# Turning and splitting the first batch's keys and values while the sorted projection still runs

## The reference, cut to what matters

```python
x = x + 0.5 * _L0_ffn_ref(_layernorm(x), ...)      # stage 1
x = x + _L0_attn_ref(_layernorm(x), ...)
x = x + 0.5 * _L0_ffn_ref(_layernorm(x), ...)      # stage 3

def _L0_ffn_ref(x, ...):
    q = _fff(x, q_...); k = _fff(x, k_...); v = _fff(x, v_...)
    attn = jax.nn.softmax(jnp.einsum('bqd,bkd->bqk', q, k) * scale, axis=-1)
    return jnp.einsum('bqk,bkd->bqd', attn, v)
```

## Time and profile before

| | |
|---|---|
| device time, median of 3 runs | 3100.54 us (3093.82 to 3103.66) |
| the profiled execution: time / span | 3108.3 us / 3106.5 us |
| mean granted clock of PE | 0.952 |
| PE busy over the span | 2852.1 us (92%) |
| DVE / ACT busy | 2122.3 us (68%) / 1796.1 us (58%) |
| stage 1's last projection tile to its first scores | 275.54 to 288.00 us |
| stage 3's last projection tile to its first scores | 2651.80 to 2665.11 us |

### The profile page before, as it was taken

One profiled execution on the slowest core, in us unless ns is written; L12 is line 12 of the kernel. 1 busy time (PEld: TensorE's weight loads), 2 busy tenths in 40 slices (PEclk: granted clock), 3 DMA queues, 4 the chain that ended last, 5 costly groups with the idle time before them and its releaser, 6 DMA issues. The chain is left out here.

```text
span 3106.5 us, 56586 instructions
## 1 busy us (share of the span) xinstructions
PE 2852.1 (92%) x20840; PEld 1746.5 (56%) x20840; DVE 2122.3 (68%) x3283; ACT 1796.1 (58%) x3505; POOL 909.7 (29%) x1482
## 2 busy tenths in 40 slices
PE   5788999998789999999999999999695589899999
PEld 2666888886543333333333333333253377688888
DVE  4445555445589999999999999998144444455544
ACT  3345443334238888888888888888544244444333
POOL 4542310001353333333333333311112554230000
PEclk8998999998769999999999999999887799999999
DMA  7785211105945544445555554332224489220110
GB/s 247 247 279 165 65 41 31 31 24 185 283 54 67 65 60 56 60 60 63 67 67 67 67 66 56 49 49 28 84 95 143 152 281 284 74 63 30 31 31 21
DMA packets 447482, 302.14 MB, mean 97 GB/s; under 512 B 170840, under 2 KB 421820, under 8 KB 447212
## 3 DMA queue, kind: packets, MB, share of 16 engines
q1 hardware_dynamic: 413292, 214.59, 35.2%
q0 software_dynamic: 33920, 83.93, 8.5%
HBM read 183.27 MB, written 118.78 MB: 97 GB/s over the span
## 5 line engine op out<-in xcount | busy, mean ns | idle before, releaser
L1564 DVE TENSOR_REDUCE mx_ha<-s_ps_ha 128x2 f32<-128x1024 f32 x1024 | 1243.6, 1222 | 59.5 <-PE s_ps_ha L1471 52.7
L1629 ACT ACTIVATE probs_ha<-s_ps_ha 128x512 f32<-128x512 f32 x2048 | 1108.8, 595 | 193.6 <-PE s_ps_ha L1482 59.5
L1471 PE MATMUL s_ps_ha<-ks_ha,qs_ha 48*128 48x512 f32 x2048 | 759.8, 455 | 15.9 <-POOL onesr_ha L1437 9.8
L1482 PE MATMUL s_ps_ha<-qs_ha,ks_ha 50*128 50x512 f32 x2048 | 749.5, 446 | 0.8 <-ACT probs_ha L1629 0.2
L1493 PE MATMUL o_ps_ha<-probs_ha,vs_ha 128*32 128x256 f32 (+1 forms) x7936 | 646.7, 398 | 0.9 <-DVE oT_ha L1591 0.9
L1471 PEld LDWEIGHTS s_ps_ha<-ks_ha,qs_ha 48*128 48x128 f32 x2048 | 313.1, 190 | 443.4 <-DVE mx_ha L1564 373.8
L896 ACT ACTIVATE probsT_a<-pT_ps_a 128x512 fp32r<-128x512 f32 x256 | 146.4, 597 | 424.3 <-PE pT_ps_a L770 409.4
L1493 PEld LDWEIGHTS o_ps_ha<-probs_ha,vs_ha 128*32 128x32 f32 x7936 | 156.5, 108 | 359.7 <-issue 185.9
L1482 PEld LDWEIGHTS s_ps_ha<-qs_ha,ks_ha 50*128 50x128 f32 x2048 | 304.6, 185 | 33.1 <-ACT probs_ha L1629 32.6
L725 POOL DMA_INDIRECT rows_a<-ys_d,slots x96 | 91.0, 948 | 634.6 <-PE turn_ps_a L747 582.0
L1421 POOL TENSOR_TENSOR onorm_ha<-oT_ha,rinv_ha 128x256 f32<-128x256 f32 x32 | 20.0, 625 | 838.4 <-DVE rinv_ha L1594 838.4
(11 more groups left out here) (215 smaller groups left out, 3958.6 us busy)
## 6 DMA issues: line engine op xcount, KB each, us to landing
xs_p<-xs_d SPq DMA_DIRECT2D x282, 128.0 KB
ys_d<-y_p SPq DMA_DIRECT2D x66, 512.0 KB
qs_ha<-parts_d SPq DMA_DIRECT2D x192, 128.0 KB, 6.1
ks_ha<-parts_d SPq DMA_DIRECT2D x192, 128.0 KB, 6.8
parts_d<-parts_hp POOLq DMA_DIRECT2D x32, 512.0 KB, 7.8
xs_d<-y_p SPq DMA_DIRECT2D x6, 1024.0 KB
leaf_w_p<-in_wa SPq DMA_DIRECT2D x4, 1048.0 KB
leaf_w_p<-in_wb SPq DMA_DIRECT2D x4, 1040.0 KB
```

What stands on the lines that cost most here:

```text
L1471: nc.tensor.matmul(s1_ps[:, e % BANKS, :], qs[0:QKROWS, n % SLOTS, c, :], ks[0:QKROWS, n % SLOTS, g * 4:(g + 1) * 4, :].rearrange("p c t - ...
L1482: nc.tensor.matmul(out, ks[LOW:LOW + KR, n % SLOTS, c, :], qs[LOW:LOW + KR, n % SLOTS, g * 4:(g + 1) * 4, :].rearrange("p c t -> p (c t)") ...
L1564: nc.vector.reduce_max(mx[:, at:at + 2], s1_ps[:, e % BANKS:e % BANKS + 2, :], AX_X).then_inc(s1_free, 1)
L1629: nc.scalar.activation(probs[:, (n + c) % (LATE + 1), g * 512:(g + 1) * 512], s2_ps[:, turn % TURNS, :], ACT.Exp).then_inc(s2_free, 1)
```

## The change

In the last tiles of the projection the same engines now turn and split the first batch's keys, one key tile in every second tile from tile 102 (`turn_k`, `k_up`, `k_low`), and split its values, one in each of the last 16 tiles (`v_up`, `v_low`). The transposes use the PSUM banks of `route_ps` and `rank_ps`. The attention block no longer does either, and begins with `turn(FQ, 0)`. The split keys `k0T` are now allocated outside, at the addresses at which `xn` lay, so the first `k_up` waits until every scatter has landed. The gathers of the values are paced at 3 tiles for 2 gathers instead of 2 for 1, and `early_rows` is two semaphores, one for keys and one for values.

```diff
+        TURN_AT, SPLIT_AT = 2 * SEG + 8, NT - QT
+        turn_in = {TURN_AT + 2 * t: t for t in range(QT)}
+        split_in = {SPLIT_AT + t: t for t in range(QT)}
+        def turn_bank(t):
+            return (route_ps, rank_ps)[t % 2][:, 0:D]
...
-                    pool.wait_ge(turned, (i + 2) * SEG - 12 + t if i == 0 else 2 * SEG + 4 + 2 * t)
+                    pool.wait_ge(turned, (i + 2) * SEG - 12 + t if i == 0 else 2 * SEG + 4 + 3 * t // 2)
...
+            def k_low(t):
+                dve.wait_ge(turn_high, t + 1)
+                parts = k0T[:, :, :, t * P:(t + 1) * P]
+                nc.vector.tensor_tensor(parts[:, 1], turn_bank(t).rearrange("p (c t) -> p c t", c=C),
+                                        parts[:, 0].bitcast(F32), ALU.subtract).then_inc(turn_split, 1)
+            def v_low(t):
+                dve.wait_ge(v_high, t + 1)
+                nc.vector.tensor_tensor(v0[:, t, 1], v0[:, t, 1].bitcast(F32), v0[:, t, 0].bitcast(F32),
+                                        ALU.subtract).then_inc(v_split, 1)
...
                     nc.vector.tensor_copy(y[:, g % YB, j % GROUP], y_ps[:, n % 2, 0:D]).then_inc(y_copied, 1)
+                    if n in turn_in:
+                        k_low(turn_in[n])
+                    if n in split_in:
+                        v_low(split_in[n])
...
+            def k_up(t):
+                act.wait_ge(row_turned, t + 1)
+                if t == 0:
+                    for f in range(FF):
+                        act.wait_ge(scattered[f], 16 * GT)
+                nc.scalar.activation(k0T[:, 0, :, t * P:(t + 1) * P], turn_bank(t).rearrange("p (c t) -> p c t", c=C),
+                                     ACT.Identity).then_inc(turn_high, 1)
+            def v_up(t):
+                if t == 0:
+                    act.wait_ge(early_rows[1], 16 * QT)
+                nc.scalar.activation(v0[:, t, 0], v0[:, t, 1].bitcast(F32), ACT.Identity).then_inc(v_high, 1)
...
+            def turn_k(t):
+                if t == 0:
+                    pe.wait_ge(early_rows[0], 16 * QT)
+                if t >= 2:
+                    pe.wait_ge(turn_split, t - 1)
+                for c in range(C):
+                    last = nc.tensor.transpose(turn_bank(t)[:, c * P:(c + 1) * P],
+                                               k_rows[:, t * D + c * P:t * D + (c + 1) * P], ident[:, :])
+                last.then_inc(row_turned, 1)
...
                     before_at = at
+                    if n in turn_in:
+                        turn_k(turn_in[n])
...
-            for t in range(QT):
-                turn(FK, t)
             turn(FQ, 0)
             scores(0)
```

More of the change, by code:

```diff
@@ L66, in rows_of, with fff_project @@
     return dram[bass.ds(t * TOK, TOK), :].rearrange("(s p) d -> p s d", p=P)
-def fff_project(nc, tag, sem, x_in, w, ident, slots, k1T, v0, xs_d, ys_d, fill):
+def fff_project(nc, tag, sem, x_in, w, ident, slots, xn, k0T, k1T, v0, xs_d, ys_d, fill):
     GT = N // P
@@ L95, in fff_project @@
         eps, warm = sb("eps", [P, 1]), sb("warm", [P, 1])
-        xn = sb("xn", [P, GT, D])
         xT = sb("xT", [P, 2, C, TOK])
@@ L143, in fff_project @@
         filled = [sem(f"filled{f}") for f in range(FF)]
-        early_rows = ctx.enter_context(nc.semaphore(f"early_rows_{tag}"))
+        early_rows = [ctx.enter_context(nc.semaphore(f"early_rows{k}_{tag}")) for k in range(2)]
         scattered = [ctx.enter_context(nc.semaphore(f"scattered{f}_{tag}")) for f in range(FF)]
@@ L152, in fff_project @@
         y_stored = [sem(f"y_stored{k}") for k in range(YB)]
+        row_turned, turn_high, turn_split = sem("row_turned"), sem("turn_high"), sem("turn_split")
+        v_high, v_split = sem("v_high"), sem("v_split")
         loads = [(ident[:, :], w["ident"]), (node_w[:, :, :], w["node_w"]), (node_b[:, :], w["node_b"]),
@@ L275, in _ @@
                 for t in range(QT):
-                    pool.wait_ge(turned, (i + 2) * SEG - 12 + t if i == 0 else 2 * SEG + 4 + 2 * t)
+                    pool.wait_ge(turned, (i + 2) * SEG - 12 + t if i == 0 else 2 * SEG + 4 + 3 * t // 2)
                     dst = k_rows[:, t * D:(t + 1) * D] if f == 1 else v0[:, t, 1, :].bitcast(F32)
                     pool.indirect_dma_start(dst, None, ys_d[f],
-                                            bass.IndirectOffsetOnAxis(slots[:, f, t:t + 1], 0)).then_inc(early_rows, 16)
-            pool.wait_ge(early_rows, 16 * 2 * QT)
+                                            bass.IndirectOffsetOnAxis(slots[:, f, t:t + 1], 0)).then_inc(early_rows[i], 16)
+            for i in range(2):
+                pool.wait_ge(early_rows[i], 16 * QT)
         @block.vector
@@ L502, in _ @@
                     copy_turned(n + 2)
+                if n in turn_in:
+                    k_up(turn_in[n])
+                if n in split_in:
+                    v_up(split_in[n])
         @block.tensor
@@ L630, in _, with fff_attend @@
                     before_at = at
+                    if n in turn_in:
+                        turn_k(turn_in[n])
                 second_layer(NT - 1, before_at)
-def fff_attend(nc, tag, sem, x_in, ident, slots, k1T, v0, ys_d, x_out):
+def fff_attend(nc, tag, sem, x_in, ident, slots, k0T, k1T, v0, ys_d, x_out):
     STEPS = B * QT
@@ L696, in fff_attend @@
         kT = [k0T, k1T]
-        k_rows = k1T[:, :, :, :].rearrange("p h c t -> p (h c t)").bitcast(F32)
-        AHEAD = 1 + QT
         def turn_bank(n):
-            return s_ps[:, n % KG, 0:D] if n < AHEAD else turn_ps[:, 0:D]
+            return s_ps[:, 0, 0:D] if n == QT else turn_ps[:, 0:D]
         block = ctx.enter_context(nc.Block())
@@ L736, in turn @@
                 n = turn_of[g]
[L737 to L742, removed]
+                pe.wait_ge(gathered[nth[g] % RR], 16 * (nth[g] // RR + 1))
+                row = rows[:, nth[g] % RR, :]
+                if n > QT + 1:
                     pe.wait_ge(turn_split, n)
-                elif KG <= n < AHEAD:
-                    pe.wait_ge(turn_split, n - KG + 1)
                 for c in range(C):
@@ L848, in close @@
                                                ALU.mult, ALU.add).then_inc(out_ready, 1)
-            for t in range(QT):
-                turn_low(FK, t)
             turn_low(FQ, 0)
@@ L857, in _ @@
                 low_part(i, 1)
-                if i == 0:
-                    for t in range(QT):
-                        v_low(t)
                 for g in turns_of(i):
@@ L896, in high_part @@
                 nc.scalar.activation(probsT[:, 0, g, :], pT_ps[:, g % 2, :], ACT.Identity).then_inc(pT_high, 1)
-            for t in range(QT):
-                turn_up(FK, t)
             turn_up(FQ, 0)
@@ L905, in _ @@
                 high_part(i, 1)
-                if i == 0:
-                    for t in range(QT):
-                        v_up(t)
                 for g in turns_of(i):
@@ L1949, in feed_forward @@
                 ident = both.enter_context(nc.sbuf_tensor(f"ident_{which}", [P, P], F32))
-                k1T = both.enter_context(nc.sbuf_tensor(f"k1T_{which}", [P, 2, C, S], F32R))
+                with nc.sbuf_tensor(f"xn_p{which}", [P, N // P, D], F32) as xn:
+                    pass
+                k0T, k1T = (both.enter_context(nc.sbuf_tensor(f"{n}_{which}", [P, 2, C, S], F32R)) for n in ("k0T", "k1T"))
                 v0 = both.enter_context(nc.sbuf_tensor(f"v0_{which}", [P, QT, 2, D], F32R))
-                fff_project(nc, f"p{which}", sem, x_in, w, ident, slots, k1T, v0, xs_d, ys_d, which == 1)
-                fff_attend(nc, f"a{which}", sem, x_in, ident, slots, k1T, v0, ys_d, x_out)
+                fff_project(nc, f"p{which}", sem, x_in, w, ident, slots, xn, k0T, k1T, v0, xs_d, ys_d, which == 1)
+                fff_attend(nc, f"a{which}", sem, x_in, ident, slots, k0T, k1T, v0, ys_d, x_out)
         feed_forward(1, x, x1)
```

3 lines of the change are left out of this document (1 added, 2 removed).

## The result

The changed kernel took 3104.15 us in the median of 12 runs, the kernel before 3095.22 in the median of 12 beside it. The ratio is 1.0023 with a 95% interval of 1.0013 to 1.0033, so 7.1 us slower (4.0 to 10.2). The time lies in the forecast range, but the direction was not forecast: I expected the parts to cancel to -0.2 us. The profiled execution took 3104.2 us, less than the one of before, so the single profiles can't show this loss as a whole; single executions spread by 10 us and more. What they do show is read stage by stage, and it came again in a second profile of the changed kernel, each stretch within 2 us.

What follows compares the result with a forecast made beforehand. PE bounds the projection, while the attention's start and step 0 hold waits and a cold clock. Gains of 16.7 us less costs of 16.5 gave -0.2, so a 3100 us median, with an 8-in-10 range of 3090 to 3108.

Steps and rivals of the forecast that it cites:

- A: Attention's start: key turns leave, the first turn waits for its query gather; gain 3.5 / 3.9 us in stages 1 / 3.
- B: Attention's first scores: start at 1.2 GHz after the pause, costing 2.25 / 0.65 us in stages 1 / 3, together 2.9.
- C: Attention's step 0: without the value splits PE's wait for DVE goes; gain 4.65 us each stage, together 9.3.
- D: Projection: turns of 16 key tiles are paid in full on PE, 3.5 us each stage, together 7.0.
- E: Projection's last tiles: DVE's splits push out the weights' copy, costing 3.3 us each stage, 6.6 in all.
- the DMA rival: Projection tiles 98 to 120: faster value gathers make DMA queues fall behind, 6.6 us each stage, 3113 us; chance 0.08.

Runs made afterwards that it cites:

- the later start: The kernel before with its first value gather due at 104 turned tiles, then one for 2 tiles as before: ratio 0.9984 against the kernel before.
- keys alone: Changed kernel with value splits back in step 0, only keys turned in the projection, value gathers from 104 turned tiles at the old rate: ratio 1.0000 against before.

## Why the prediction was wrong

By its own steps, each for one stage, the mean over two profiles of the changed kernel and two of before (its own and the one with only the addresses changed), both stages:

| step | forecast | measured |
|---|---|---|
| A, start of the attention | -3.7 | -3.4 (12.8 to 9.3 us) |
| B, cold first scores | +1.45 | +1.6 (10.8 to 12.4) |
| C, step 0 | -4.65 | -4.6 (20.5 to 15.9) |
| D, PE's turns | +3.5 | +3.1 (97 to 140 with the later start: keys alone 50.1, before 47.0) |
| E, DVE's splits | +3.3 | +1.5 (124 to 140: 19.5 - 17.2, less 4 turns of 0.19) |
| the gathers | 0 | +4.1 (what is left) |

From tile 97 to 140 the means are 58.2 and 49.5 us, +8.7, of which D and E make 4.6. The rest, 4.1, I put down to the gathers' new pace, with its cold clock. It is a remainder and no measurement: alone the pace brought 2.65 a stage, and the terms don't simply add, since turns are hidden where gathers slow the tiles. The sum is +2.3 a stage, 4.6 in all, inside the measured 4.0 to 10.2 but below its middle of 7.1.

A, B, C and D were right in mechanism and near in size (A's gather took 2.80 us from issue to the turn, 286.57 to 289.37, where I had 2.35). B also settles what was weighed against a page: the scores lost about what the clock's rows had said. By the Trainium skill ("TensorE: Matmul & The Clock Gate", Part 4, PE-mode transpose) the transposes would not have warmed them and B would be 0. The trace does not agree: B is 1.6 us a stage, and in the kernel before the clock rose to 1.00 with nothing but transposes on PE since the pause.

E was over-sized. The chain from a result's copy to the next weights' copy is real, but the pair of tiles took 0.24 us more than PE's own work, where I had 0.35 + 0.21. The likely reason, not tested, is that I added the deficit of every tile as if none passed its slack on to the next.

The step that failed is the sentence under the DMA rival: "284 KB per us at the new mean of 1.20 us a tile, against 128 + 128 + 64 in 1.09 = 294 now, which ran through; so PE's own slowing should prevent it". It failed twice. It is an average, and the gathers don't come evenly: POOL first waits until the values' last stores have landed, by then 101 or 102 tiles are turned, and what is due then and in the next tile or two goes out back to back, four or five gathers instead of three. The pace alone, with no work moved, made the kernel 5 us slower, most of what the sum lacked. And what "ran through" did not: the kernel before already paused there (tiles 97 to 101 in 5.6 and 6.0 us against 4.4 without a burst), which its own trace would have shown, but the stretch that I read began at 232, behind nearly all of the pause (in stage 1 the copies of tiles 99 and 100 start at 229.15 and 232.07). Nor does one gather a tile run through there: under the key gathers, tiles 80 to 96 of the kernel before take 23.8 and 22.9 us, some 1.45 each, so what the earlier trace rows shows of one pause is the smaller part. The rival had the right place and sign, a price of 6.6 us a stage (2.65 for the pace alone, 4.1 as what is left here), and too small a chance.

One sign came true by luck. The stretch from tile 102 to the last was to grow by 6.8 us and grew by 6.5 (41.7 to 48.2), but D and E make only 4.6 of that; the gathers brought the rest, and another 2.3 ahead of tile 102, where I had not looked.

What stays open: which transfer it is that comes late behind the burst. The trace puts the late results down to PE, to "remote" and to "issue", with no landing time for SP's loads and stores. The queues that bring the engines' own instructions (q8 and q14) have one transfer each between 226 and 236 us too, and no run rules them out.

## What to carry to other kernels

Before moving work to another stage, try another order where it stands: a few small pieces ahead of one that PE waits for cost 4.6 us a stage, and putting them behind it gave about 3.6 of that back without touching the projection. When a pace of background DMAs is set by a counter, look at the counter's value at the moment when the queue is first free to run, since everything overdue goes at once; and check the stretch in which they start, not only the average bandwidth. A stage in which PE is the bound pays nearly in full for every transpose that is moved into it (0.19 us of 0.22 here), while the place it leaves may then wait for a DMA and a cold clock.

## What the hardware showed that I had not expected

Five indirect gathers of 128 KB let go at once under loaded queues made a result on DVE 4 us late; behind a pause of 3 us the clock was at 0.50 for 4 us (232 to 236), and tiles that PE does in 1.09 us took twice that. Raising the rate of such gathers from one in 2 tiles to 4 in 5, in groups of two or three back to back, slowed 16 tiles from 17.6 to 22.1 us, though the DMA engines moved less in them (264 GB/s against 288). The buffers' addresses made no difference that could be measured (0.9984 to 1.0005).
